# Splitting the load of z in the second layer: za and the reversed rows an iteration earlier, the padded copy on a semaphore of its own

## What is computed

```python
spatial = conv_general_dilated(x, conv_spatial_w, padding 1)            # 3x3, 128 -> 128 channels
spectral = irfft2(W @ rfft2(x))                                         # a 1x1 mix of the spectrum
# mamba: 256 inner channels, 16 states each, over the 4096 pixels in order
xc = silu(causal_conv4(in_proj(u)))
dt = softplus(dt_proj(x_proj(xc)[:8]))
h  = exp(dt * A) * h + dt * B * xc                                      # the scan, for each channel and state
y  = (sum over states of h * C + D * xc) * silu(gate)
out = spatial + spectral + out_proj(y)
```

## Time and profile before

| | |
|---|---|
| median of 3 executions | 6187.24 us (6182.13 to 6188.05) |
| the profiled execution | 6181.0 us, its span 6179.2 us |
| busy over the span | PE 90%, DVE 79%, POOL 67%, ACT 60% |
| first layer | up to about 3950 us |
| second layer, 32 iterations | about 4005 to 6175 us |
| DVE in the second layer | 9 tenths or more in nearly all slices |
| DMA in the second layer | 4 tenths busy, about 150 GB/s |

### The profile page before, as it was taken

The page is one execution under the profiler, slowest core; times in us unless marked ns, Lnnn a source line. Parts: engine busy times, 40 slices in busy tenths (PEclk is TensorE's granted clock), DMA queues, the critical chain, the costliest instruction groups (busy, mean ns, idle before and its releaser), DMA issues. The chain is left out here.

```text
span 6179.2 us, 90944 instructions
## 1 busy us (share of the span) xinstructions
PE 5589.3 (90%) x27184; PEld 2550.2 (41%) x27184; DVE 4912.2 (79%) x7188; ACT 3717.1 (60%) x7290; POOL 4118.1 (67%) x3147
## 2 busy tenths in 40 slices
PE   7999999999999999999999999677777777777777
PEld 3444444444444444444444444233333333333332
DVE  7777777777777777777777777299999999999998
ACT  3666666666656666666666666566566656666665
POOL 2677766676766677666677776376676666676776
PEclk9999999999999999999999999899899889988998
DMA  4011011111110110110100000244444444444444
GB/s 132 20 42 40 29 31 34 32 43 30 32 35 25 38 42 29 40 33 23 31 18 12 21 9 21 67 164 144 157 150 143 153 151 148 142 157 149 146 153 144
DMA packets 293852, 465.18 MB, mean 75 GB/s; under 512 B 73680, under 2 KB 97104, under 8 KB 291920
## 3 DMA queue, kind: packets, MB, share of 16 engines
q1 hardware_dynamic: 293360, 459.70, 23.4%
HBM read 381.74 MB, written 76.28 MB: 74 GB/s over the span
## 5 line engine op out<-in xcount | busy, mean ns | idle before, releaser
L560 POOL TENSOR_TENSOR sums<-exps 128x512 f32<-128x512 f32 x2048 | 2617.3, 1299 | 1312.5 <-ACT exps L493 1307.8
L569 DVE TENSOR_REDUCE mpart<-ps 128x1 f32<-128x512 f32 x4096 | 2539.7, 682 | 820.3 <-PE ps L369 820.3
L493 ACT ACTIVATE exps<-ps 128x512 f32<-128x512 f32 x4096 | 2127.9, 603 | 1405.0 <-PE ps L376 1404.6
L1224 POOL TENSOR_TENSOR hc<-hh,c_rep 128x512 f32<-128x512 f32 x1024 | 1422.0, 1393 | 713.1 <-DVE hh L1195 710.7
L369 PE MATMUL ps<-k_st,q_ring 96*128 96x512 f32 x4096 | 1754.1, 429 | 18.4 <-DMA k_st<-qk_split 9.3
L376 PE MATMUL ps<-q_ring,k_st 98*128 98x512 f32 x4096 | 1621.4, 397 | 4.0 <-ACT exps L493 3.6
L1195 DVE TENSOR_TENSOR_SCAN hh<-d_a,carry,ps 128x512 f32<-128x512 f32 x1024 | 1296.0, 1268 | 1.0
L369 PEld LDWEIGHTS ps<-k_st,q_ring 96*128 96x128 f32 x4096 | 774.6, 189 | 1065.0 <-DVE mpart L569 548.7
L387 PE MATMUL ps<-exps,v_ring 128*32 128x512 f32 x8192 | 1090.8, 605 | 0.0
L1016 PE MATMUL ps<-s_u,sel_g 128*128 128x512 f32 x1024 | 665.6, 650 | 232.6 <-DVE hh L1195 230.5
L376 PEld LDWEIGHTS ps<-q_ring,k_st 98*128 98x128 f32 x4096 | 778.3, 190 | 148.2 <-ACT exps L493 17.3
(11 more groups left out here) (106 smaller groups left out, 2906.1 us busy)
## 6 DMA issues: line engine op xcount, KB each, us to landing
d_a<-dt_dram SPq DMA_DIRECT2D x1040, 256.0 KB
qk_split<-hilo SPq DMA_DIRECT2D x128, 256.0 KB, 2.3
q_ring<-qk_split SPq DMA_DIRECT2D x384, 64.0 KB, 2.0
k_st<-qk_split SPq DMA_DIRECT2D x45, 512.0 KB, 7.0
dt_dram<-dt SPq DMA_DIRECT2D x33, 512.0 KB, 2.8
za<-z_ext SPq DMA_DIRECT2D x33, 320.0 KB, 6.1
zp<-z_ext SPq DMA_DIRECT2D x33, 320.0 KB, 8.0
xc<-in_x SPq DMA_DIRECT2D x32, 256.0 KB, 3.1
```

The costliest lines, as they stand in the source:

```text
L493: nc.scalar.activation(exps[:, u % 4, CH * half:CH * half + CH], a_bank(("exp", n, t)), ACT.Exp, scale=SCALE).then_inc(a_done, 1)
L560: pool.tensor_tensor(sums[:, u % 8, :], exps[:, u % 4, 0:CH], exps[:, u % 4, CH:2 * CH], ALU.add).then_inc(summed, 1)
L569: nc.vector.tensor_reduce(mpart[:, m % 2, t % 4, t // 4:t // 4 + 1], d_bank(("max", m, t)), AX.X, ALU.max).then_inc(d_done, 1)
L1224: pool.tensor_tensor(hc[:, g % NHC, :], hh[:, g % NHH, :], c_rep[:, p, :], ALU.mult).then_inc(hc_ready, 1)
```

## The change

`load` no longer takes the padded copy with it. `za` and the two pieces of `stage_j` are loaded at step 6 of iteration j-2, where they were loaded at step 26, behind waits for `item` (all ten products of the chunk that lay in this buffer of za have been made) and `flipped`. The padded copy has a function of its own, `load_padded(j)`, called at step 8 of iteration j-1, and a semaphore `zp_in`, for which PE waits ahead of the first convolution matmul (g = 18). ACT waits for `z_used` itself before it writes zj, since the load behind it no longer does.

```diff
--- before.py
+++ after.py
@@ -811,10 +811,10 @@
                 nc.vector.tensor_tensor(row0[:, 0, 0:1], row0[:, 0, 0:1], cols[:, 7:8], ALU.add)
         clear(nc, names)
 
-        (z_in, flipped, item, item_read, sp_log, dt_sum, u_prod, hi_ready, lo_ready,
+        (z_in, zp_in, flipped, item, item_read, sp_log, dt_sum, u_prod, hi_ready, lo_ready,
          u_rep, da_ready, bu_ready, scanned, kept, hc_ready, y_done, y_added, gated, z_used, o_ready, o_copied,
          o_full, o_even, o_odd, dt_stored) = [sem(x) for x in (
-             "z_in", "flipped", "item", "item_read", "sp_log", "dt_sum", "u_prod",
+             "z_in", "zp_in", "flipped", "item", "item_read", "sp_log", "dt_sum", "u_prod",
              "hi_ready", "lo_ready", "u_rep", "da_ready", "bu_ready", "scanned", "kept", "hc_ready", "y_done",
              "y_added", "gated", "z_used", "o_ready", "o_copied", "o_full", "o_even", "o_odd", "dt_stored")]
         dt_in = [sem(f"dt_in{i}") for i in range(NDA)]
@@ -853,19 +853,23 @@
         with nc.Block() as block:
             @block.sync
             def _(sp):
-                def load(j, p):
-
-                    jw = j % NIT
-                    b, lc = jw // STEPS, jw % STEPS
-
-                    ge(sp, z_used, j - 1)
+                def load(j):
+
+                    p, b, lc = j % 2, j % NIT // STEPS, j % STEPS
+                    if j >= 2:
+                        sp.wait_ge(item, (j - 2) * NITEM + GI + 1)
                     ge(sp, flipped, 2 * j)
                     sp.dma_start(za[:, p, :], z_ext[b, :, bass.ds(lc * LC, HALO)]).then_inc(z_in, 16)
-                    sp.dma_start(zp[:, p, :, 1:W + 1], z_ext[b, :, bass.ds(lc * LC, HALO)].rearrange("c (h w) -> c h w", w=W)).then_inc(z_in, 16)
 
                     last = (STEPS - 1 - lc) * LC + W
                     sp.dma_start(stage_j[:, 0:ROWS - 1, :], z_ext[b, :, bass.ds(last + W, LC - W)].rearrange("c (h w) -> c h w", w=W)).then_inc(z_in, 16)
                     sp.dma_start(stage_j[:, ROWS - 1, :], z_ext[b, :, bass.ds((STEPS - lc) % STEPS * LC + W, W)]).then_inc(z_in, 16)
+
+                def load_padded(j):
+
+                    p, b, lc = j % 2, j // STEPS, j % STEPS
+                    ge(sp, z_used, j - 1)
+                    sp.dma_start(zp[:, p, :, 1:W + 1], z_ext[b, :, bass.ds(lc * LC, HALO)].rearrange("c (h w) -> c h w", w=W)).then_inc(zp_in, 16)
 
                 def store(j, p):
                     b, lc = j // STEPS, j % STEPS
@@ -896,11 +900,14 @@
                             load_dt(it + 1, 1 - p, t + NDA - G)
                         if t == 18 and it:
                             store(it - 1, 1 - p)
-                        if t == 26 and it + 2 <= NIT:
-                            load(it + 2, p)
-
-                load(0, 0)
-                load(1, 1)
+                        if t == 6 and it + 2 <= NIT:
+                            load(it + 2)
+                        if t == 8 and it + 1 < NIT:
+                            load_padded(it + 1)
+
+                load(0)
+                load_padded(0)
+                load(1)
                 store_dt(0, 0)
                 for g in range(NDA):
                     load_dt(0, 0, g)
@@ -912,7 +919,7 @@
                 sp.wait_ge(o_odd, 16 * (NIT // 2))
                 for i in range(NDA):
                     sp.wait_ge(dt_in[i], 16 * (NIT * G // NDA + 1))
-                sp.wait_ge(z_in, 64 * (NIT + 1))
+                sp.wait_ge(z_in, 48 * (NIT + 1))
 
             @block.tensor
             def _(pe):
@@ -927,7 +934,7 @@
 
                     if 1 <= g <= 7:
                         if g == 1:
-                            pe.wait_ge(z_in, j * 64 + 64)
+                            pe.wait_ge(z_in, j * 48 + 48)
                         for n in (g - 1,) if g < 7 else (6, 7):
                             h, k = n // 4, n % 4
                             if k == 0:
@@ -977,6 +984,7 @@
                         if n == 0:
 
                             ge(pe, o_copied, it)
+                            pe.wait_ge(zp_in, it * 16 + 16)
                         dy, dx = n // 3, n % 3
                         nc.tensor.matmul(o.rearrange("p (a b) -> p a b", b=W), wconv[:, n, :], zp[:, p, dy:dy + ROWS, dx:dx + W],
                                          start=(n == 0), stop=False)
@@ -1061,7 +1069,8 @@
                 def prepare(j, p, g):
                     if g == 3:
 
-                        act.wait_ge(z_in, j * 64 + 64)
+                        act.wait_ge(z_in, j * 48 + 48)
+                        ge(act, z_used, j - 1)
                         zf = zj[:, p, :].rearrange("p (h w) -> p h w", w=W)
                         nc.scalar.copy(zf[:, :, 0:1], stage_j[:, ::-1, 0:1]).then_inc(flipped, 1)
                         nc.scalar.copy(zf[:, :, 1:W], stage_j[:, ::-1, W - 1:0:-1]).then_inc(flipped, 1)
```

## The result

The changed kernel takes 6093.5 us (median of 4; 6093.2 to 6097.0) where the one before takes 6187.7 us (median of 4 in the same comparison; 6182.1 to 6198.2). The ratio is 0.9847, with a 95% interval of 0.983 to 0.9864: faster by 94 us. The forecast was 6128 us with a range from 6114 to 6145. The direction was right and the size wasn't; the gain is 1.6 times the 59 us of the sum, and outside the range.

What follows compares the result with a forecast made beforehand. DVE bounds the second layer, idle ahead of the product with B where PE waits for z; 56.6 + 2.4 = 59 us go, 6181 - 59 = 6122, plus 6.2 to the median: 6128 us, range 6114 to 6145.

Steps and rivals of the forecast that it cites:

- the 59 us of the sum: DVE's expected gain in the second layer: 56.6 us of gaps ended by PE plus 2.4 us from PE's low clock.
- The parts costed at nothing: Moved loads on SP, PE's wait for zp, ACT's wait for `z_used` and the start: each forecast to cost 0.
- The slack of 16 us: On SP, d_a loads for groups 23 to 31 behind z's transfers: about 16 us to spare before DVE is late.
- The two kinds of transition: Between iterations: 17 without a branch, where DVE waits for PE and z; 14 with one, where it waits for code.
- number 3 of the count: DVE's gaps without a releaser, mostly ahead of the product with B: all 69.7 us of "issue" stay.
- number 2: DVE's second gaps behind branches: 2.9 us taken as its own, 2.2 us more stays, only 0.7 us goes.
- The stops at the branch get shorter too: Rival at the 14 branches back: stops shrink by 4 to 11 us more, giving 6117 to 6124 us; chance 0.17.
- The line through ACT's 5.54 us at 0.91 and DVE's 4.70 us at 0.54: At the branch, stop against DMA share: 2.3 us per unit of share, so 14 stops would gain 4 us.
- The upper end: Bound on shorter branch stops: the shortest, 3.87 us, taken for all 14 of mean about 4.65, gains 11 us.
- the 6.2 us between it and the median: Whole kernel: median of 6187.2 us lies 6.2 us above the profiled 6181.0 us; added to 6122 for the forecast.
- The 6 us by which z was to hold SP: On SP, z's transfers ahead of the d_a loads: 0.4 + 0.4 + 4.8 + 0.4 = 6 us of holding.
- one sign: PE at transitions: it would no longer run at half clock there if the forecast held.

Runs made afterwards that it cites:

- the last experiment: The changed kernel with d_a loads of steps 25 to 31 held back before 14 branches and issued together behind step 1 of the next iteration: 6056.9 us.

## Why the prediction was right, and where it failed

**Right.** DVE's gaps of 3.1 us ahead of group 2 were z's, and they went: 58.1 us where gaps and intervals had given 57 to 59. An iteration without a branch takes 63.14 us, against 63.24 forecast. The parts costed at nothing cost nothing: PE's wait for zp and ACT's for `z_used` don't appear, and ACT's wait for d_a is 7.6 us. The slack of 16 us fits what was seen: DVE bore up to 15 us more of holding and not 27. The two kinds of transition, told apart by the place of the gap, were the right reading, and the loop written out confirms that the one kind is the branch's.

**The step that failed** is number 3 of the count, "The 69.7 us of "issue" stay", and with it the "0.74 us" of number 2 that I took "as DVE's own". They didn't stay: 53.4 us are left, and the small gap is gone. Per branch 1.7 us went, 23.8 us in all, where the sum had 0.7 us for all 14: 13.0 us of it in the first gap (64.6 to 51.6 us over the 14), 7.8 us in the second (9.5 to 1.7 us), the rest in smaller ones.

**Why it failed.** I had the cause at hand as a rival, "The stops at the branch get shorter too", with 4 to 11 us. Both its ends were wrong in kind:
- The line through ACT's 5.54 us at 0.91 and DVE's 4.70 us at 0.54 took the DMA share as the measure. But 0.5 is what the engines show with the loads of d_a one behind the other, and it was the share in the stop that I read: 0.54 before the change and 0.47 after it, hardly a difference. The difference lies ahead of the stop, where the share was 0.73 before (5078.40 to 5081.40) and is 0.52 after, and behind the stop. After the change the backlog ends during DVE's stop (share 0.10 just behind it), and the second gap is gone. The one branch of 69.7 us fits: there the share stays at 0.52 behind the first stop, and the second gap comes.
- The upper end took "the shortest, 3.87 us", and the first gap alone. All 14 stops of before ran through the same backlog of z and d_a (share 0.68 to 0.75 in the 3 us ahead of each); the shortest of them says nothing on a stop without it. The 0.9 us of the last experiment is that. And the 7.8 us of the second gap stood in neither end.
- A stop with no releaser was taken for a constant, where the packets above show a transfer at its end. The rule of the Trainium skill on the fetch behind a taken branch (the section named above) pointed the right way and the runs agree with it, but I gave it only the price of my line.

**The other terms.** 3.5 us came at the start of the layer: PE's wait for z of chunk 0 ended 3.8 us after the issue of za rather than 5.3 us (1.5 us, with zp no longer ahead), 1.1 us came before the layer's own work began and has nothing to do with the change, and PE's first matmuls were 0.8 us shorter. The last 7 us of the 94 are the choice of the profiled execution: the forecast carried the 6.2 us between it and the median over to the changed kernel, where they aren't. The kernels in which PE waits for z in each iteration spread over 12 to 24 us (16 for the one before in its comparison), the changed kernel over 4 us; so part of z's delay seems to fall out anew in each execution, and a sum made against one of the fastest is short. The 6 us by which z was to hold SP are now about 1.7 us, since the large piece of stage_j, 4.78 us in the earlier trace rows, is issued in 0.43 us in the median; that changed nothing. And one sign was wrong without harm: PE's granted clock still falls at a transition without a branch (0.63 in the mean from 4838.00 to 4842.00, between its two levels), and the transition takes 63.14 us all the same. The low clock alone costs DVE nothing there.

**Still open.** Why z comes later in the kernel before when its loop is written out, what makes its pieces slow at step 26, and whether the queues of the DMA engines or the memory behind them hold up the code's transfer. No run tells these apart.

## What to carry to other kernels

The gaps with no releaser right behind this hardware loop's branch end with a transfer of code. Their length depended on what the DMA engines held at that moment, so whoever moves bulk loads away from such a loop's end or towards it may change them, and writing the loop out removed them (54 us of 6094 here). Where a loop is to be judged, look for packets of the kind "instruction" ahead of the gap's end. Where a transfer is issued matters more than what stands ahead of it in its own group: the same small piece of z took 4.2 us at one step and 9.3 us at another, right behind a burst of other loads. And before pricing a stop by the shortest one in the trace, ask whether any of those seen was free of what is to be removed.

## What the runs showed of the hardware that I had not expected

- DVE's stop at the branch back: 4.7 us and 0.74 us with z and d_a in the DMA queues, 3.7 us with d_a alone, 0.9 us with the DMA engines idle. Three more transfers of 320 KB added no more than one (6110 us, and 6111 to 6115 us).
- DVE went on 2.0 to 2.5 us behind the last packet of the kind "instruction" in nearly all of these stops, whatever their length.
- 320 KB in rows of 2560 bytes delayed the code about as much as in rows of 256 bytes (6111.0 and 6114.8 us).
